# A graph network on one core: waits at the heads of quads, ring groups of 8 tiles, row copies in late quads, key one-hots for four units

## What is computed

```python
def gatv2_layer(x, src, dst, Wl, Wr, att, bias, n_nodes, heads):
    xl = (x @ Wl).reshape(N, heads, Dh)
    xr = (x @ Wr).reshape(N, heads, Dh)
    e = jax.nn.leaky_relu(xl[src] + xr[dst], NEG_SLOPE)
    logits = jnp.einsum('ehd,hd->eh', e, att)
    m = jax.ops.segment_max(logits, dst, num_segments=n_nodes)
    a = jnp.exp(logits - m[dst])
    denom = jax.ops.segment_sum(a, dst, num_segments=n_nodes)
    alpha = a / denom[dst]
    out = jax.ops.segment_sum(alpha[:, :, None] * xl[src], dst, num_segments=n_nodes)
    return out.mean(axis=1) + bias
...
h = jax.nn.relu(gatv2_layer(x, src, dst, W1l, W1r, att1, b1, N, 8))
h = gatv2_layer(h, src, dst, W2l, W2r, att2, b2, N, 4)
x = _layernorm(x + h)
...
agg = jax.ops.segment_sum(x[src], dst, num_segments=x.shape[0])
h = x + agg
h = jax.nn.relu(h @ W1 + b1)
h = jax.nn.relu(h @ W2 + b2)
x = _layernorm(x + h @ W3 + b3)
```

## Time and profile before

| what | value |
| --- | --- |
| median of 3 runs | 3819.62 us (3816.06 to 3821.36) |
| profiled execution, its own time | 3812.78 us |
| its span in the profile | 3811.0 us |
| PE busy | 3136.0 us (82% of the span) |
| DVE busy | 2677.0 us (70%) |
| POOL busy | 2500.8 us (66%) |
| ACT busy | 1944.4 us (51%) |

### The profile page before, as it was taken

One profiled execution on the slowest core, in us unless ns is written; L12 is line 12 of the kernel. 1 busy time (PEld: TensorE's weight loads), 2 busy tenths in 40 slices (PEclk: granted clock), 3 DMA queues, 4 the chain that ended last, 5 costly groups with the idle time before them and its releaser, 6 DMA issues. The chain is left out here.

```text
span 3811.0 us, 89063 instructions
## 1 busy us (share of the span) xinstructions
PE 3136.0 (82%) x31400; PEld 1856.8 (49%) x31400; DVE 2677.0 (70%) x6673; ACT 1944.4 (51%) x5497; POOL 2500.8 (66%) x1949
## 2 busy tenths in 40 slices
PE   0369999999999999994629799797997978559886
PEld 0235555555555555553515455453554535347663
DVE  3538888888888888886745466464664647489972
ACT  3346556666665666651306455454554544158761
POOL 4488787687687687406378888888888870557620
PEclk9989999999999999996759899898998988579997
DMA  3323333333333333214222233232332322211210
GB/s 62 59 51 75 79 82 82 76 88 83 75 84 80 75 90 82 70 53 100 57 46 63 58 74 75 61 75 60 70 75 61 75 60 44 40 32 38 44 41 22
DMA packets 417512, 249.11 MB, mean 65 GB/s; under 512 B 258173, under 2 KB 380449, under 8 KB 416562
## 3 DMA queue, kind: packets, MB, share of 16 engines
q0 software_dynamic: 97392, 70.80, 10.8%
q10 hardware_dynamic: 237600, 89.88, 9.3%
q1 hardware_dynamic: 82086, 82.74, 8.7%
HBM read 135.21 MB, written 105.95 MB: 63 GB/s over the span
## 5 line engine op out<-in xcount | busy, mean ns | idle before, releaser
L1011 PE MATMUL L_e_ps_z<-L_e_xT,L_w_abs 128*128 128x500 f32 x2700 | 1382.6, 622 | 193.1 <-ACT L_e_rl L1127 192.3
L598 POOL DMA_INDIRECT L_e_tiles<-in_x_dram,src_tile x800 | 1107.9, 1385 | 350.3 <-issue 234.1
L598 POOL DMA_INDIRECT L_e_tiles<-x_d,src_tile x800 | 1010.2, 1263 | 250.2 <-issue 237.7
L1127 ACT ACTIVATE L_e_rl<-L_e_ps_z 128x500 f32<-128x500 f32 x1350 | 778.8, 586 | 573.0 <-PE L_e_ps_z L1011 571.0
L1319 DVE SCALAR_TENSOR_TENSOR L_e_acc<-L_e_acc,L_e_row,L_e_ps_v 128x130 f32<-128x130 f32 (+1 forms) x1440 | 447.4, 311 | 620.2 <-PE L_e_ps_v L1073 434.4
L1011 PEld LDWEIGHTS L_e_ps_z<-L_e_xT,L_w_abs 128*128 128x128 f32 x2700 | 444.7, 191 | 480.1 <-issue 370.1
L642 ACT ACTIVATE L_e_xs<-L_e_tiles 125x64 f32 x1800 | 308.8, 248 | 390.1 <-issue 255.6
L1073 PEld LDWEIGHTS L_e_ps_v<-L_e_xs,L_e_p 125*64 125x64 f32 x8400 | 318.3, 141 | 357.8 <-issue 175.8
L1073 PE MATMUL L_e_ps_v<-L_e_xs,L_e_p 125*64 125x65 f32 x8400 | 425.8, 235 | 19.4 <-DVE L_e_acc L1319 15.5
L1118 ACT ACTIVATE L_e_xT<-L_e_ps_x 128x500 f32<-128x500 f32 x450 | 264.8, 588 | 236.5 <-PE L_e_ps_x L998 236.4
L1230 DVE SCALAR_TENSOR_TENSOR L_e_f<-L_e_rl,L_sign,L_e_f 128x500 f32<-128x500 f32 x450 | 329.1, 731 | 9.9 <-ACT L_e_rl L1127 6.6
(11 more groups left out here) (323 smaller groups left out, 4211.0 us busy)
## 6 DMA issues: line engine op xcount, KB each, us to landing
L_v_d<-L_e_acc ACTq DMA_DIRECT2D x225, 260.0 KB
L_e_dlb<-dloc_d SPq DMA_DIRECT2D x90, 468.8 KB, 5.1
L_v_d<-L_e_acc ACTq DMA_DIRECT2D x225, 130.0 KB
L_e_tiles<-in_x_dram,src_tile POOLq DMA_INDIRECT x800
L_e_tiles<-x_d,src_tile POOLq DMA_INDIRECT x800
L_e_lim<-limits_d SPq DMA_DIRECT2D x180, 39.1 KB
L_max_d<-L_e_me SPq DMA_DIRECT2D x45, 78.1 KB
L_e_lim<-limits_d SPq DMA_DIRECT2D x180, 19.5 KB
```

What stands on the lines that cost most here:

```text
L598: pool.indirect_dma_start(lay.tiles[:, g % TR * D:(g % TR + 1) * D], None, lay.x_rows, bass.IndirectOffsetOnAxis(k.src_tile[:, g:g + 1], 0 ...
L1011: pe.matmul(ps_z[part % ZR][:, 0:QT], lay.w_abs[:, part * 128:(part + 1) * 128], xT[q][:], start=True, stop=True).then_inc(s["z_ready"], 1)
L1127: act.activation(rl[n % NE][:], ps_z[part % ZR][:, 0:QT], ACT.Relu, scale=1.0 - SLOPE).then_inc(s["relu_done"], 1)
```

## The change

It has four parts.

- Ring groups of 8 tiles instead of 16: `TF`, the shift in `need_i`, the mask in `counts`, and the ranges of `fetch_tiles`, so that as many tiles are gathered ahead as before.
- PE in the edge pass: the waits on `xT_ready`, on `p_ready` of a quad's first sums and on `chain` of its first pair move to the head of `body`, ahead of `turn`. `turn` loses its wait on `xT_ready` for the quad before. Part 0 of `project` waits for the relus of the whole quad before, and part 1 waits for nothing.
- ACT in layer 2 (`lay.norm`): the wait for rows and the load of places move from body q = 0 to q = 2; the copies of groups 0 and 1 are made at q = 2, 2 and 3 at q = 3, 4 at q = 4. Tiles `f`, which layer 2 doesn't use, are no longer allocated there.
- Neighbour sums: `ohk` is built for four units at once as `[125, 200, 4]`, by a comparison of two bf16 tensors, 256 of them instead of 1024 comparisons with a scalar. Two new copies on DVE build the operands `keys4` and `key16` once. The count matmul reads its moving operand with a step of four elements. The ring of `ohk` has 3 such tiles instead of 10 small ones.

```diff
@@ -62,12 +62,12 @@
...
 TR = 64
-TF = 16
+TF = 8
 NF = G // TF
...
 LR = 8
-FETCHED = (2, 4)
+FETCHED = (4, 8)
 assert UT % CU == 0 and BLK % CU == 0 and UT % BLK == 0 and N % T == 0 and E % T == 0 and U % R == 0 and NT % TG == 0 and UT // BLK % BG == 0 and G % BLK == 0 and GU % GR == 0 and G % TF == 0 and TR % TF == 0 and CU == 20
@@ -374,7 +374,7 @@
...
                 units(dve.tensor_scalar(ring_off[:], ring_off[:], float(D), None, ALU.mult))
-                units(dve.tensor_scalar(need_i[:], gidx[:], 4, None, ALU.arith_shift_right))
+                units(dve.tensor_scalar(need_i[:], gidx[:], 3, None, ALU.arith_shift_right))
                 units(dve.tensor_copy(last_u[:], key_all[0:1, TF - 1:G:TF]))
@@ -582,7 +582,7 @@
...
     eng.load(regs, places)
-    return [(eng.snap(r, donate=True, min_val=0, max_val=63) & 63) + 1 for r in regs]
+    return [(eng.snap(r, donate=True, min_val=0, max_val=127) & 127) + 1 for r in regs]
@@ -738,7 +738,7 @@
...
-                fetch_tiles(k, pool, lay, 0, 2)
+                fetch_tiles(k, pool, lay, 0, 4)
@@ -888,7 +888,7 @@
...
         rl = [sbuf(nc, ctx, f"{nm}rl{r}", [128, QT]) for r in range(NE)]
-        f = [sbuf(nc, ctx, f"{nm}f{r}", [128, QT]) for r in range(3)]
+        f = [sbuf(nc, ctx, f"{nm}f{r}", [128, QT]) for r in range(0 if lay.norm else 3)]
         lg = [sbuf(nc, ctx, f"{nm}lg{r}", [128, SL]) for r in range(3)]
@@ -986,8 +986,6 @@
...
                         pe.wait_ge(s["oht_ready"], c.val(1, 1))
-                    if c.after(1) or q >= 2:
-                        pe.wait_ge(s["xT_ready"], c.val(NQ, q - 1))
                     ps = ps_x[(c.slot(2) * NQ + q) % 2]
@@ -1004,9 +1002,9 @@
...
                     g = c.slot(XR) * NQ + q
-                    if part == 0:
-                        pe.wait_ge(s["xT_ready"], c.val(NQ, q + 1))
-                    if c.after(1) or C * q + part >= ZR:
+                    if part == 0 and (c.after(1) or q):
+                        pe.wait_ge(s["relu_done"], c.val(NQ * C, q * C))
+                    if part > 1:
                         pe.wait_ge(s["relu_done"], c.val(NQ * C, q * C + part - ZR + 1))
@@ -1064,9 +1062,9 @@
...
                     st = c.slot(XR) * Q + u // NQ
-                    if u % NQ == 0:
+                    if n and u % NQ == 0:
                         pe.wait_ge(s["p_ready"], c.val(Q, u // NQ + 1))
-                    if n % 2 == 0 and (c.after(1) or u >= 4):
+                    if n == 2 and (c.after(1) or u >= 4):
                         pe.wait_ge(s["chain"], c.val(CU, u - 2))
@@ -1081,10 +1079,17 @@
...
                 def body(c, q):
+                    zc, zq = lag(c, q, 1)
+                    bc, bq = lag(c, q, 15)
+                    if (c.after(1) or q >= 1) and zc.there():
+                        pe.wait_ge(s["xT_ready"], zc.val(NQ, zq + 1))
+                    if c.after(3) and bc.there():
+                        if Q * bq % NQ == 0:
+                            pe.wait_ge(s["p_ready"], bc.val(Q, Q * bq // NQ + 1))
+                        if bc.after(1) or bq:
+                            pe.wait_ge(s["chain"], bc.val(CU, Q * bq - 2))
                     if c.there():
                         turn(c, q, blocks)
-                    zc, zq = lag(c, q, 1)
-                    bc, bq = lag(c, q, 15)
                     rc, rq = lag(c, q, 3)
@@ -1183,11 +1188,12 @@
...
                     if one.there():
-                        if q == 0:
+                        if q == (2 if lay.norm else 0):
                             if one.after(XR):
...
                             places[:] = row_places(act, lay, one)
-                        copy_rows(act, lay, one, places, q)
+                        for row_q in (((), (), (0, 1), (2, 3), (4,))[q] if lay.norm else (q,)):
+                            copy_rows(act, lay, one, places, row_q)
                     zc, zq = lag(c, q, 1)
@@ -1643,7 +1649,7 @@
...
                 pool.iota(wins_i[:], [[1, Q], [Q, NW]], base=0, channel_multiplier=0).then_inc(s["iota"], 1)
-                fetch_tiles(k, pool, lay, 2, lay.fetched)
+                fetch_tiles(k, pool, lay, 4, lay.fetched)
@@ -1726,13 +1732,15 @@
...
     PAIRS = GR_U // 2
-    HR, KR, CR, PQ = 3, 10, 3, 4
+    HR, KR, CR, PQ = 3, 3, 3, 4
     W4 = WN * D // Q
...
         winhot8 = sbuf(nc, octx, nm + "winhot8", [BU, EB, Q, NW])
+        keys4 = sbuf(nc, octx, nm + "keys4", [T, KEYS, HU], BF16)
+        key16 = sbuf(nc, octx, nm + "key16", [T, EU], BF16)
         x3 = sbuf(nc, octx, nm + "x3", [T, NT, 3, D], BF16)
@@ -1749,6 +1757,8 @@
...
                 def _(dve):
+                    dve.tensor_copy(keys4[:], keys_n[:].unsqueeze(2).to_broadcast([T, KEYS, HU]))
+                    dve.tensor_copy(key16[:], key_of[:])
                     dve.wait_ge(s["part"], 1)
@@ -1758,7 +1768,7 @@
...
             ohr = [sbuf(nc, ctx, f"{nm}ohr{r}", [T, RW, HU], BF16) for r in range(HR)]
-            ohk = [sbuf(nc, ctx, f"{nm}ohk{r}", [T, KEYS], BF16) for r in range(KR)]
+            ohk = [sbuf(nc, ctx, f"{nm}ohk{r}", [T, KEYS, HU], BF16) for r in range(KR)]
             cnt = [sbuf(nc, ctx, f"{nm}cnt{r}", [T, NT, GR_U, EN], BF16) for r in range(CR)]
@@ -1842,7 +1852,7 @@
...
                             v = 2 * n + u
-                            pe.matmul(ps_c[n % 2][0:RW, u * KEYS:(u + 1) * KEYS], ohr[v // HU % HR][:, :, v % HU], ohk[v % KR][:],
+                            pe.matmul(ps_c[n % 2][0:RW, u * KEYS:(u + 1) * KEYS], ohr[v // HU % HR][:, :, v % HU], ohk[v // HU % KR][:, :, v % HU],
                                       start=True, stop=True).then_inc(s["counted"], 1)
@@ -1933,10 +1943,12 @@
...
-                    def hot_keys(v):
-                        if v >= KR:
-                            dve.wait_ge(s["counted"], v - KR + 1)
-                        dve.tensor_scalar(ohk[v % KR][:], keys_n[:], key_of[:, v:v + 1], None, ALU.is_equal).then_inc(s["hot"], 1)
+                    def hot_keys(g):
+                        if g >= KR:
+                            dve.wait_ge(s["counted"], (g - KR + 1) * HU)
+                        dve.tensor_tensor(ohk[g % KR][:], keys4[:],
+                                          key16[:, g * HU:(g + 1) * HU].unsqueeze(1).to_broadcast([T, KEYS, HU]),
+                                          ALU.is_equal).then_inc(s["hot"], HU)
@@ -1956,7 +1968,7 @@
...
                                 hot_rows((i * GR_U + u) // HU)
-                            hot_keys(i * GR_U + u)
+                                hot_keys((i * GR_U + u) // HU)
                             if u == 3 and i + 1 in gathered_in:
```

## The result

The changed kernel takes 3861.63 us (median of 5 runs, 3854.75 to 3863.57) against 3819.62 (5 runs, 3815.65 to 3822.50) before: a ratio of 1.0109, 95% interval 1.0095 to 1.0124. It is 42 us slower where 57 us faster was forecast. The profiled execution has a span of 3859.8, 48.8 more than before. The kernels further down ran on five chips, each beside the kernel before, and on three of these chips, called disturbed from here on, every kernel, the one before too, took 2.4 to 6% longer than on the other two and scattered more.

A forecast was written before the change was run, and what follows sets the result against it. Layer 1 was taken as bound by PE's matmuls, layer 2 by POOL's gathers, neighbour sums by DVE. Waits 0, ring groups in layer 1 -4, layer 2's end -20, key one-hots -33: -57, from 3819.6 to 3762 us, range 3750 to 3775.

The forecast's parts named there:

- PE's waits, 0: Edge pass: moving PE's waits to the heads of quads changes nothing, since they are satisfied with room; term 0.
- rival 1: Layer 1: the 0.10 between x' and sums is the wait and goes away, 23 to 31 us; chance 0.10.
- a late DVE chain that now stops x' too: Edge pass: the whole quad queues behind PE's head wait, x' first; with 2.8 us of room, not late.
- forecast -4: Layer 1, ring groups of 8: chunks 1 to 4 gain 2.2 us and chunk 8 about 2.
- the 2.2 us: Layer 1, chunk 4: row copies can't start before 297.6, against 299.79 now; this gain stays.
- forecast 12.1 at the end: End of layer 2: chunk 43 needs 792 tiles instead of 800, so its rows can be copied 12.1 us earlier.
- In the middle of the pass both parts only move idle time from one quad to another: Layer 2: ring groups and late row copies gain only after the last gather; no size given for the middle.
- the pace of POOL stays: Layer 2: gathers keep starting 1.51 us apart, so the pass can only gain after the last gather, 3133.63.
- DVE's price: Neighbour sums: one comparison for four units steps by 0.49 instead of 0.72, shortening DVE's turn from 5.03 to 4.1 us.
- the next limits: Neighbour sums: turns then last 4.70 us with a block (PE) and 4.28 without (ACT); stage term -33.
- I take the lower end: Neighbour sums, PE: a count matmul reading columns 8 bytes apart costs what it does now, 0.085 us each.
- rival 2: Neighbour sums: strided counts cost 0.17 (total 3824) or up to 0.25 (3900); chance 0.08 at about twice, 0.06 above.

The follow-up runs named there:

- without the key part: The changed kernel with the neighbour sums of before (key one-hots unit by unit), other three parts kept: 3804.48 us, 0.9974 of the kernel before.
- the kernel with ring groups and two units: The kernel before with ring groups of 8 and key one-hots for two units, on an undisturbed chip: 3784.52 us, ratio 0.9916.
- the two-unit kernel: The kernel before with key one-hots for two units in one comparison, interleaved at a step of 4 bytes: 3801.14 us, ratio 0.9969.
- The flat layout: The kernel before with four units' key one-hots in one comparison, laid out one unit after the other: 3883.04 us, ratio 1.0192.

## Why the prediction was wrong, step by step

- **PE's waits, 0.** Right for layer 1: x' to sums 0.52 and z to sums 1.87 are as in the earlier trace rows, and rival 1 is out. From the first to the last xT copy of layer 1 it is 1489.5 and 1488.0 us in two kernels with ring groups and these waits (the changed one, and without the key part), and 1488.0 and 1489.6 in the two with ring groups without them. Wrong that they are worth nothing anywhere: they move DVE's work against the gathers, by some 25 us for the better beside late copies. On disturbed chips they lose 0.3 to 1.3%. The prediction names a mechanism that fits, a late DVE chain that now stops x' too, but no run takes it apart.
- **Ring groups.** Layer 1: forecast -4, measured -4.7, and that is luck. The row copies of chunk 4 came as worked out (298.1 for 297.6), but the 2.2 us did not stay: its first xT copy is at 331.79, and was at 331.64 before. The whole gain came from short stalls that are gone at chunks 8 and 9 (2.9 us together), 17 and 18 (1.3), 26 and 35 (1.2), of which I had priced one. Layer 2: forecast 12.1 at the end. In the kernel with ring groups and two units the last gather is 56.0 us before the last xT copy, 67.8 before: 11.8.
- **Late row copies.** The step that failed is "In the middle of the pass both parts only move idle time from one quad to another", and with it "the pace of POOL stays". What they gain behind the last gather is there (in the changed kernel from the copies at 3139.28 to xT 13.3 us, for 13.8), but the moved idle time moves DVE's scans against the gathers, and the pass runs at the pace of gathers. The page of before had the sign: a gather of layer 2 takes 1263 ns in the mean, and 1.21 us in every row that the prediction shows.
- **Key one-hots.** DVE's price was right (0.48 for 0.49), and the next limits too, as the two-unit kernel shows with turns of 4.18 and 4.75 for 4.28 and 4.70. The step that failed is the price of the strided moving operand, "I take the lower end": 0.17 a count, the value of rival 2, which had a chance of 0.08, and not 0.085. My reason for the low end, that weights are read with the same step at no cost, doesn't carry over to the moving operand. The Trainium skill, "SBUF — State Buffer", section "Specifications (TRN2)", has full bandwidth for two hits in a line of 16 bytes, and so for this step; the traces do not agree, 0.17 for 0.085, and the measurement decides. Rival 2 then was too cheap, 28 for 53: I priced its turns at 6.1 and 5.2, they are 6.15 and 5.42, and late blocks add 9 us in five turns (up to 10.3; behind the wait in that one the granted clock is 0.50 from 3609 to 3613). Where the first two pairs of a turn have no multiply beside them, ACT's 0.52 a tile stands in PE's way, and I had left that out.
- **Even two-unit one-hots bring 11 us and not 33.** In that kernel ten turns of 5.4 to 9.3 us hold 25 us more than turns of 4.18 and 4.75 would. In most of them PE waits for transfers, and its granted clock is lower behind the wait. In the kernel with ring groups and two units, the waits of PE, and a block after one:

```profile
PE g_ps_w L1877 <- DMA g_blk<-sum_d: 10.9, 6, 3.4
PE g_ps_p L1870 <- DMA g_xs<-x_d,src_idx: 7.2, 3, 2.8
...
3409.38 1.25 PE L1877 MATMUL g_ps_w<-g_blk,g_winhot 128*98 128x512 f32 x2 [3.10 <-DMA g_blk<-sum_d]
3410.41 0.54 PE L1849 MATMUL g_ps_c<-g_ohk,g_ohr 125*128 125x200 bf16 x2
```

  The granted clock is 1.00 up to 3410.0, 0.50, the lower of its two levels, from 3410.4 to 3413.5, and 0.99 from there to 3420. At the lower level pairs step by 0.34 from 3410.41 on, though their operand has a step of 4 bytes; the pair of 3414.06 is back at 0.18. I allowed 3 us for late gathers and nothing for block loads.

The sum: instead of 0 - 4 - 20 - 33 = -57 the two traces have about 0 - 5 (layer 1) - 20 (end of layer 2) + 19 (its gathers) + 53 (neighbour sums) and +1 or 2 elsewhere = +49, the difference of the spans. Of the 106 us between the two sums 86 are the neighbour sums and 19 the gathers of layer 2.

## What to carry to other kernels

Price a layout twice, for the engine that writes it and for the one that reads it: an interleave that saves the writer a third can cost the reader half its rate, and the step at which that begins is worth one small run. Where an engine that bounds a stage shares something with another, moving the other's work in time is a change of price, not a free edit: ask where the moved work falls in the bounding engine's cycle, above all when both are tied together by a flag. Here two parts of four were worth keeping, ring groups of 8 and one-hots for two units, and together they beat the kernel before by 0.8%, on an undisturbed chip.

## What the runs showed of the hardware

- A matmul with a bf16 moving operand of 200 columns takes 0.086 us at a step of 2 bytes, 0.092 at 4 and 0.17 at 8, at a granted clock of 1.00. At the lower level the step of 8 bytes costs nothing: the first four counts of the stage, behind an idle stretch of PE and at a granted clock of 0.50 in both traces, take as long in the changed kernel as before.

```profile
3362.49 0.88 PE L1855 MATMUL g_ps_c<-g_ohk,g_ohr 125*128 125x200 bf16 x4 [32.06 <-DVE g_ohk L1949]
```

```profile
3368.29 0.89 PE L1845 MATMUL g_ps_c<-g_ohk,g_ohr 125*128 125x200 bf16 x4 [31.91 <-DVE g_ohk L1939]
```

  An estimate from these: 200 columns 8 bytes apart in 0.171 us are 9.4 bytes passed in a ns, and 4 bytes apart in 0.092 are 8.7, so some 9 bytes a ns, with 0.086 as the least that 200 columns take. No larger step was run.
- A comparison of two bf16 tensors of 800 elements steps by 0.91 when one operand has a step of zero inside, and by 0.48 where the repeated dimension is outside. The flat layout is the only one run with such a step, and its inner dimension is longer too (200 for 4).
- One DVE scan of 1.45 us lengthens an indirect gather by nothing to 1.2 us, by where in the gather's cycle of 1.51 us it starts: a gather that starts under a scan ends 1.02 us behind the scan's end instead of 1.21 behind its own start, if that is later, and one that was under way first is not lengthened.
